# A four-layer graph network in fp32: low parts made for 2048 columns at once, high parts too in the four passes, half groups finished 16 substeps apart

## The reference, cut to what matters

```python
h = relu(layernorm(x)); x = x + (adj/rowdeg) @ h @ W_in + (adj.T/coldeg) @ h @ W_out
h = relu(layernorm(x)); x = x + silu(adj @ silu(adj @ h @ W + b) @ W + b)     # two products
h = relu(layernorm(x)); x = x + relu((adj+I) normalized by 1/sqrt(deg), @ h @ W + b)
h = relu(layernorm(x)); x = x + relu((adj+I) normalized by 1/sqrt(deg), @ (h @ W) + b)
```

## Time and profile before

| | |
|---|---|
| median of 3 runs | 1160.49 us (1159.23 to 1161.83) |
| the profiled execution | 1157.68 us, span in the trace 1155.9 us |
| PE busy | 1122.3 us, 97% of the span |
| DVE busy | 1047.3 us, 91% |
| ACT busy | 893.3 us, 77% |
| granted TensorE clock | 0.999 of full speed |
| transfers | 407.40 MB on one queue, 92.4% of the time of 16 DMA engines |

### The profile page before, as it was taken

One profiled execution on the slowest core, in us unless ns is written; L12 is line 12 of the kernel. 1 busy time (PEld: TensorE's weight loads), 2 busy tenths in 40 slices (PEclk: granted clock), 3 DMA queues, 4 the chain that ended last, 5 costly groups with the idle time before them and its releaser, 6 DMA issues.

```text
span 1155.9 us, 14026 instructions
## 1 busy us (share of the span) xinstructions
PE 1122.3 (97%) x5120; PEld 918.7 (79%) x5120; DVE 1047.3 (91%) x1419; ACT 893.3 (77%) x1265; POOL 48.0 (4%) x40
## 2 busy tenths in 40 slices
PE   4999999999999899999999999999999999999997
PEld 4677888888876678888888887878887888888886
DVE  5899999989999998998987999999989999998885
ACT  6888787788778868787777778788777878777663
POOL 0000000000000000000000211201112011100000
PEclk9999999999999999999999999999999999999999
DMA  9999999999988879999999899998999999998994
GB/s 327 338 346 373 361 400 390 353 391 397 357 316 302 308 289 378 382 396 376 392 362 357 316 390 341 354 387 333 365 340 349 370 341 359 358 385 358 368 349 177
DMA packets 58244, 408.28 MB, mean 353 GB/s; under 512 B 6464, under 2 KB 7488, under 8 KB 9024
## 3 DMA queue, kind: packets, MB, share of 16 engines
q1 hardware_dynamic: 58176, 407.40, 92.4%
HBM read 405.27 MB, written 2.10 MB: 352 GB/s over the span
## 4 chain that ended last, share of the span: by engine, by line
PE 73%; DVE 18%; ACT 5%; DMA 2%; issue 2%; ACTq 0%; DVEq 0%
PE bank L605 46%; PE bank L609 23%; DVE a_lo L386 12%; PE bank L616 2%; ACT a_hi L271 2%; DMA raw<-in_adj_dram 1%; PE bank L637 1%; ACT act_raw L304 1%; DVE stats L416 1%; DVE x_sb L483 1%; ACT a_hi L269 1%; DVE h_lo L409 1%; ACT act_raw L295 1%; DMA raw<-in_adj_t_dram 1%; DVE zt L391 1%
## 5 line engine op out<-in xcount | busy, mean ns | idle before, releaser
L386 DVE TENSOR_TENSOR a_lo<-raw,a_hi 128x1024 fp32r<-128x1024 f32 x768 | 899.3, 1218 | 84.2 <-ACT a_hi L269 57.6
L269 ACT ACTIVATE a_hi<-raw 128x1024 fp32r<-128x1024 f32 x512 | 510.6, 1051 | 114.4 <-DMA raw<-in_adj_t_dram 112.9
L605 PE MATMUL bank<-a_hi,h_hi 128*128 128x512 f32 x1536 | 480.5, 394 | 15.5 <-ACT a_hi L271 15.4
L609 PE MATMUL bank<-a_lo,h_hi 128*128 128x512 f32 x1536 | 480.0, 394 | 10.5 <-DVE a_lo L386 8.9
L605 PE MATMUL bank<-a_hi,h_lo 128*128 128x512 f32 x1536 | 474.6, 390 | 0.0
L609 PEld LDWEIGHTS bank<-a_lo,h_hi 128*128 128x128 f32 x1536 | 284.3, 188 | 88.7 <-DVE a_lo L386 32.3
L605 PEld LDWEIGHTS bank<-a_hi,h_hi 128*128 128x128 f32 x1536 | 284.5, 189 | 74.1 <-DVE h_lo L409 14.6
L605 PEld LDWEIGHTS bank<-a_hi,h_lo 128*128 128x128 f32 x1536 | 288.9, 188 | 61.6
L271 ACT ACTIVATE a_hi<-raw 128x1024 fp32r<-128x1024 f32 x256 | 268.4, 1051 | 49.7 <-DMA raw<-in_adj_dram 25.1
L304 ACT ACTIVATE act_raw<-x_sb,lnbias,lnscale 128x128 f32<-128x128 f32 x96 | 39.7, 484 | 40.0 <-DVE lnbias L444 40.0
L251 POOL TENSOR_TENSOR std<-mv,eps_sb 128x4 f32<-128x4 f32 x16 | 17.4, 1087 | 936.1 <-DVE mv L420 936.1
(11 more groups left out here) (50 smaller groups left out, 183.0 us busy)
## 6 DMA issues: line engine op xcount, KB each, us to landing
raw<-in_adj_t_dram SPq DMA_DIRECT2D x320, 1024.0 KB, 6.7
raw<-in_adj_dram SPq DMA_DIRECT2D x64, 1024.0 KB, 7.0
x_sb<-in_x_dram SPq DMA_DIRECT2D x4, 512.0 KB, 11.2
out_dram<-x_sb SPq DMA_DIRECT2D x8, 256.0 KB, 6.6
w_sb<-in_L_gnn_W_dram SPq DMA_DIRECT2D x3, 64.0 KB, 12.8
b_sb<-in_L_gnn_b_dram SPq DMA_DIRECT2D x3, 64.0 KB, 10.8
w_sb<-in_L_gnn_W_in_dram SPq DMA_DIRECT2D x1, 64.0 KB, 13.7
w_sb<-in_L_gnn_W_out_dram SPq DMA_DIRECT2D x1, 64.0 KB, 13.3
```

The source lines that it names most:

```text
L269: act.activation(sub(a_hi, n), sub_raw(n), ACT.Copy).then_inc(sub_hi, 1)
L386: dve.tensor_tensor(sub(a_lo, n), sub_raw(n), sub(a_hi, n).bitcast(F32), ALU.subtract).then_inc(sub_lo, 1)
L605: pe.matmul(bank[half][:, :], weights, hi_a[:, half * GW:(half + 1) * GW], start=start and weights is hi_w, stop=False)
L609: last = pe.matmul(bank[half][:, :], hi_w, lo_a[:, half * GW:(half + 1) * GW], start=False, stop=stop)
```

## The change

DVE makes the low parts of two substeps (one tile) in one instruction of 2048 columns, in the units and in the passes. It stands where the low part of the odd substep stood, and waits for both high parts. ACT makes both high parts in one instruction in the passes alone, where the high part of the even substep stood; it waits until both places of the ring are free. In the units ACT's instructions stay as they are. `LATER` is 16 in the groups g = 1, 2, 3 of a pass, and stays 8 in group 0.

```diff
-        LATER = 8
+        LATER, LATER_FIRST = 16, 8
...
-        def late(at, s):
-            return [h for h in range(2) if at is not None and at + h * LATER == s]
+        def late(at, g, s):
+            return [h for h in range(2) if at + h * (LATER if g else LATER_FIRST) == s]
...
                 if m >= 4:
-                    sp.wait_ge(sub_lo, 2 * (m - 4) + 2)
+                    sp.wait_ge(pair_lo, m - 4 + 1)
...
+            def hi_pair(n):
+                act.wait_ge(tile_in[n // 2 % 4], 16 * (n // 8) + 16)
+                act.wait_ge(sub_used, n + 1 - RING + 1)
+                act.activation(pair(a_hi, n), pair_raw(n), ACT.Copy).then_inc(sub_hi, 2)
...
                     for s in range(NS):
-                        hi(n_of(sweep, g, s))
+                        if s % 2 == 0:
+                            hi_pair(n_of(sweep, g, s))
...
-            def lo(n):
-                dve.wait_ge(sub_hi, n + 1)
-                dve.tensor_tensor(sub(a_lo, n), sub_raw(n), sub(a_hi, n).bitcast(F32), ALU.subtract).then_inc(sub_lo, 1)
+            def lo_pair(n):
+                dve.wait_ge(sub_hi, n + 2)
+                dve.tensor_tensor(pair(a_lo, n), pair_raw(n), pair(a_hi, n).bitcast(F32), ALU.subtract)\
+                   .then_inc(pair_lo, 1)
...
                 for s in range(US):
-                    lo(n_of0(u, s))
+                    if s % 2 == 1:
+                        lo_pair(n_of0(u, s - 1))
...
-                pe.wait_ge(sub_lo, n + 1)
+                pe.wait_ge(pair_lo, n // 2 + 1)
```

More of the change, by code:

```diff
@@ L94, in build_gnn_stack @@
         sub_hi = sem("sub_hi")
-        sub_lo = sem("sub_lo")
+        pair_lo = sem("pair_lo")
         sub_used = sem("sub_used")
@@ L137, in sub, with pair, pair_raw @@
             return t[:, n % RING, :]
+        def pair(t, n):
+            return t[:, n % RING:n % RING + 2, :]
+        def pair_raw(n):
+            return raw[:, n // 2 % 4, :].rearrange("p (b n) -> p b n", b=2)
         def split_n(sweep, q):
@@ L260, in _, with hi @@
             act.activation(table_warm[:, :], eps_sb[:, :], ACT.Sqrt)
-            def hi(n, accum=None):
-                m = n // 2
+            def hi(n, accum):
                 if n % 2 == 0:
-                    act.wait_ge(tile_in[m % 4], 16 * (m // 4) + 16)
+                    act.wait_ge(tile_in[n // 2 % 4], 16 * (n // 8) + 16)
                 if n >= RING:
                     act.wait_ge(sub_used, n - RING + 1)
-                if accum is None:
-                    act.activation(sub(a_hi, n), sub_raw(n), ACT.Copy).then_inc(sub_hi, 1)
-                else:
-                    act.activation(sub(a_hi, n), sub_raw(n), ACT.Copy, accum_out=accum).then_inc(sub_hi, 1)
+                act.activation(sub(a_hi, n), sub_raw(n), ACT.Copy, accum_out=accum).then_inc(sub_hi, 1)
+            def hi_pair(n):
+                act.wait_ge(tile_in[n // 2 % 4], 16 * (n // 8) + 16)
+                act.wait_ge(sub_used, n + 1 - RING + 1)
+                act.activation(pair(a_hi, n), pair_raw(n), ACT.Copy).then_inc(sub_hi, 2)
             def first_std(i):
@@ L369, in _ @@
                         if ps in (1, 2):
-                            for half in late(AT_SILU[ps], s):
+                            for half in late(AT_SILU[ps], g, s):
                                 silu(ps, 2 * pg + half)
                         if ps == 1:
-                            for half in late(AT_HI[ps], s):
+                            for half in late(AT_HI[ps], g, s):
                                 split_hi(ps, 2 * pg + half)
                         if ps in (2, 3):
-                            for half in late(AT_HI[ps], s):
+                            for half in late(AT_HI[ps], g, s):
                                 ln_relu(ps, 2 * pg + half)
@@ L555, in _ @@
                     for s in range(NS):
-                        lo(n_of(sweep, g, s))
+                        if s % 2 == 1:
+                            lo_pair(n_of(sweep, g, s - 1))
                         if ps == 0:
@@ L580, in _ @@
                             continue
-                        for half in late(AT_Z, s):
+                        for half in late(AT_Z, g, s):
                             z_out(ps, 2 * pg + half)
                         if ps in (2, 3):
-                            for half in late(AT_STATS, s):
+                            for half in late(AT_STATS, g, s):
                                 if ps == 2:
@@ L588, in _ @@
                                 ln_stats(ps, 2 * pg + half)
-                            for half in late(AT_AFFINE, s):
+                            for half in late(AT_AFFINE, g, s):
                                 ln_affine(ps, 2 * pg + half)
                         if ps in (1, 2, 3):
-                            for half in late(AT_LO[ps], s):
+                            for half in late(AT_LO[ps], g, s):
                                 split_lo(ps, 2 * pg + half)
```

## The result

The changed kernel takes 1190.97 us (median of four runs, 1185.77 to 1197.62), the kernel before 1159.86 in the same comparison (four runs, 1158.70 to 1161.83): a ratio of 1.0247, interval 1.0201 to 1.0292. That is 31 us slower. The direction was forecast, the size (+2.4) and the range (up to 1169) were not. One execution further down, the profiled one of experiment 5 (1230.66 us), counts as slow and is left out of that experiment's ratio.

What follows compares the result with a forecast made beforehand. PE, busy for 97% of the span, was taken as the bound, so only its waits, about 40 us, could be given back. 4.5 + 0.5 - 2.1 - 0.5 = +2.4 us on 1160.5 gave 1162.9 us; range 1156 to 1169.

Steps and rivals of the forecast that it cites:

- The direction: Whole kernel: slower, by +2.4 us; chances slower 0.48, same 0.28, faster 0.24.
- The costs of the instructions: A pair takes 2288 ns on DVE and 1887 ns on ACT; DVE saves about 0.076 us a pair, 29 us over 384.
- Units 0 to 2: First units: pairs (6,7) and (12,13) wait behind the ReLUs, lateness is handed on; +4.5 us, bounds +2 to +6.
- 92 to 315 us: Smooth stretch: first low part comes 2.1 us later, PE's lead shrinks by 1.1 us; +0.5 us, between 0 and 3.
- The rival: 92 to 315 us: loop of four tiles starves, 2.80 us a tile against PE's 2.72, 6.4 us more, 1169; chance 0.08.
- 315 to 430 us: Last three units gain 1.2, start of pass 1 2.0, less 1.1 of lead: -2.1 us, bounds -5 to +1.5.
- Passes: Passes: a dip smaller by 2.9 us against a cushion smaller by 1.9 to 3.2; -0.5 us, between -5.9 and +3.
- The spread: Passes: halves 16 apart shrink DVE's dip, nearly nothing within the -0.5 us; rival with lighter DVE, 1155 us, chance 0.24.
- I am wrong if ... PE waits appear from 92 to 315 us: Stated refutation: PE not late at 95 us, PE waits from 92 to 315 us, or waits of the passes vanishing.

Runs made afterwards that it cites:

- experiment 5: Kernel before, no pairs; each tile load waits for one more low part before it takes its place in raw: 1210.95 us, ratio 1.0394.
- experiment 8: Changed kernel with the ReLUs of units 0 to 2 after high parts 5 and 11 instead of 6 and 12: 1192.68 us, ratio 1.0281.
- experiment 6: Changed kernel with five places in raw instead of four and a ring of six instead of eight: 1168.38 us, ratio 1.0062.
- experiment 13: Kernel before with three places in raw instead of four: 1230.75 us, ratio 1.0589.
- 7: Kernel before with five places in raw and a ring of six instead of eight: 1152.07 us, ratio 0.9921.
- 10: Kernel before with five places, a ring of six, and the halves 16 substeps apart in groups 1 to 3: 1152.88 us, ratio 0.9935.
- 12: Kernel before with five places, a ring of six, and high parts in pairs in the passes, low parts single: 1163.97 us, ratio 1.0025.
- 16: Kernel before with high pairs alone in the passes, five places, ring of eight, row sums sharing places: 1161.98 us, ratio 1.0008.
- 11: Changed kernel with five places, a ring of six, and scale and bias, ReLUs and low half of h two substeps later in passes 2 and 3: 1164.45 us.
- 14: Changed kernel, all pairs, with five places, the ring of eight, and row sums sharing places: 1172.14 us, ratio 1.0084.
- 15: Kernel before with low pairs alone, five places, ring of eight, row sums sharing places: 1185.15 us, ratio 1.0196.
- experiment 1: Kernel before with the halves 16 substeps apart in groups 1 to 3 of a pass, no pairs: 1163.3 us, ratio 1.0007.
- 9: Kernel before with a ring of six instead of eight, still four places: 1161.09 us, ratio 1.0012.
- 2: Changed kernel with LATER back at 8, pairs without the spread: 1194.98 us, ratio 1.0295.
- 4: Kernel before with high parts in pairs in the passes, low parts single, halves 8 apart: 1177.23 us, ratio 1.0136.

## Why the prediction was wrong, step by step

**The costs of the instructions: right.** 2287 ns for 2288, 1914 for 1887. The rule of the Trainium skill beside them (Perfetto Trace Analysis, Optimizing Scalar/DVE Operations), that instructions broken up may let work complete sooner, spoke against the change. The trace agrees: DVE saved 20 us and the kernel lost 31.

**"Units 0 to 2", +4.5: the right sign, two thirds of the size.** PE started the low part of substep 14 of unit 2 at 92.82, not 90.02: 2.8 late, where 4.5 was forecast (94.5). Unit 2 as it ran, on DVE and PE:

```profile
71.80 2.26 DVE L395 TENSOR_TENSOR a_lo<-raw,a_hi 128x2048 fp32r<-128x2048 f32 x1
...
78.62 2.29 DVE L395 TENSOR_TENSOR a_lo<-raw,a_hi 128x2048 fp32r<-128x2048 f32 x1 [1.99 <-ACT a_hi L274]
...
87.07 2.29 DVE L395 TENSOR_TENSOR a_lo<-raw,a_hi 128x2048 fp32r<-128x2048 f32 x1 [0.55 <-ACT a_hi L274]
```

```profile
92.82 0.74 PE L621 MATMUL bank<-a_lo,h_hi 128*128 128x512 f32 x2 [0.39 <-DVE a_lo L395]
```

The wait of 2 us before the pair (6,7) is there as forecast (1.99); before (12,13) it is 0.55 and not 1. On DVE the low parts behind unit 2's statistics began 1.25 us late (71.80 against 70.55), where the sum carried 2.55 into it (1.9 of unit 0 and 0.65 of unit 1): lateness is handed on less than assumed. Within the unit PE lost (92.82 - 71.80) - (90.02 - 70.55) = 1.6 us where the walk gave 2.1. That the ReLUs cause it was argued and isn't borne out: moved between the pairs, they gave back 0.4 us (experiment 8). PE's first matmul of units 1, 2 and 3 and of unit 4 (substep 64) came 1.9, 2.5, 2.8 and 2.9 us later than before, so two thirds of the loss arise in unit 0. The cause of these 2.9 us stays open; that the first low part of a tile now comes with the second is left, and wasn't tried alone.

**"92 to 315 us", +0.5: the step that failed.** It had the hold nearly right (4.5 us) and left out what it does to the next load. It looked at PE's lead over DVE and asked whether the 2.1 us by which a first low part comes later would use it up. It didn't close the loop through SP: the later end of the pair is also the later start of a load. The rival did close it ("if a load still takes its 6.7 us and the place is held 4.5"), gave 2.80 us a tile, and was put at 0.08, on the argument that a load had taken 5.1 us with fewer under way. Measured: load 6.99, held 4.68, 2.92 a tile, +9.7 us. Experiment 5 makes a loss of the same kind without pairs, experiment 6 takes it away with the pairs in place, experiment 13 shows why the 5.1 didn't apply. The rival's 6.4 us came out near for a wrong reason: it set its 2.80 us against 2.72, PE's time without the weight products, while PE takes 2.80 in this stretch with them, so by its own two numbers it would have cost nothing. Both were a little low (6.7 for 6.99, 4.5 for 4.68), and so was the hold before, 3.4 for 3.93, which makes the loop look as if it had 0.3 us a tile to spare ((6.7 + 3.4) / 4 = 2.5) where it had 0.04. Against before, the hold grew by 0.75 us, 72 x 0.75 / 4 = 13.5 us; the slack that was there took up 72 x 0.043 = 3.1 of them (201.28 / 72 = 2.796 less 2.753), the load that was 0.09 us shorter 72 x 0.09 / 4 = 1.6, which leaves 8.8 and, with 0.9 us unaccounted for, the 9.7.

**"315 to 430 us", -2.1: half of it.** The start of pass 1 did gain, 51.85 us for substeps 256 to 288 before and 50.39 after (-1.5; forecast -2.0 for it). The last three units lost 2.2 us (208 to 256: 80.4 to 82.6) where they were to gain 1.2. With five places the stretch takes 80.4 us in all kernels with single low parts (7, 10, 12, 16) and 81.8 in all with low pairs (6, 11, 14, 15), so 1.4 us are the low pairs' and not the loop's; why they lose is open. The remaining 0.8 us is less than by which kernels with single low parts differ there with four places (80.4 before, 82.1 in experiment 1, 82.0 in 9).

**"Passes", -0.5 with an upper bound of +3: the largest error, +25.7.** Two cushions were weighed against each other; tiles appeared only as coming 1.9 us later after landing, and the loop was again left out, though 112.9 us of waits of ACT for tiles stood in the earlier trace rows. Runs of other executions put the size at 18 to 26 us (394.8 us in experiment 8, 399.0 in 2). A fifth place gives back 16.4 (402.8 to 386.4), the later chain 4.0 (to 382.4), 9.1 are left against five places without pairs (373.3). The fifth place gives the kernel before 3.8 as well (377.1 to 373.3), so with as many places the pairs cost 13.1 of the 25.7: about half is the four places', half the pairs' own. The 9.1 weren't settled. What is shown of them: they aren't the ring (experiments 9, 14, 16), they aren't the spread (1, 10), and high pairs by themselves make as much (12, 16: 12.5 and 10.2 us). That the first low part then can't start until the whole pair of high parts is made, 0.86 us later (1914 - 1051), and that this tells in the bursts after ACT's ReLUs, fits the longer hold (5.54 us in experiment 12, 5.14 in 7) and DVE's longer waits for high parts, but was not tested alone.

**The direction.** That it came out right is in part luck: what made the forecast slower was its +4.5 us in the first units, and they made 2.9 of the 40 us of the profiled execution.

**The spread.** Forecast as part of "nearly nothing", and nothing it was (experiments 1 and 10).

**The words "I am wrong if ... PE waits appear from 92 to 315 us"** named the right place: 12.0 and 4.4 us of waits appeared. PE was late at 95 us, though less than forecast, and the waits of the passes grew instead of staying.

**POOL.** Its term was missing altogether. The Trainium skill (SBUF — State Buffer, SBUF: two separate sides) says that DVE and GpSimd share a pair of ports, held for a whole instruction and also by a DVE operation with two inputs in SBUF when GpSimd reads SBUF. The trace agrees to the nanosecond or two: POOL's operations grew by 1067 and 1066 ns, DVE's by 1069, and in the kernels with single low parts (experiments 1, 4, 7, 9, 12) they stay at 1087 to 1089 and 1866.

## What to carry to other kernels

Before making an instruction larger, write down the loop of the buffer that it reads: (load + wait + hold) / places against the consumer's time per tile. In substeps 64 to 208 that was 2.75 against 2.80 us, and holding a place 0.75 us longer cost 9.7 us there, while 20 us of DVE's time saved over the whole kernel brought nothing back; from 92 to 315 us ACT had waited 44.4 us for tiles before, beside a PE that never waited. Take the hold from the trace and not from the lengths of instructions: it was 3.93 us, not 3.4. Don't let a load shorten in the sum unless a row shows it at the same number of loads under way. And where such a loop is near, try a further place first: here it alone made the kernel 0.8% faster (0.6 to 1.0), with the ring cut to six to make room.

## What the runs showed of the hardware

- A load of 1 MB took 7.0 us with 2.4 to 2.5 under way on average (6.6 in experiment 6, with 2.4) and 5.1 us with 1.7; all the same three places move less (354 against 381 GB/s from 120 to 300 us for three and four places).
- A small POOL operation that runs beside a long DVE instruction of two inputs can grow by as much as that instruction: +1.07 us on average for each of the two when DVE's grew by 1.07. It depends on how they meet: in experiment 6 the second took 2100 ns instead of 2932.
- With loads that wait for places, executions of one kernel spread over 3 to 12 us and, in experiment 5, 32 (before 1158.70 to 1161.83 and, in 29 runs, 1157.57 to 1167.49; after 1185.77 to 1197.62); with a fifth place over 0.1 to 2.4.
- The fall in PE's busy time (4.6 us in 223) was half of the time that it lost (9.7); the count of its instructions gave the whole.
